# A selective scan on one core: C rows spread by DMA instead of TensorE, one scan over both halves, skip term and residual summed in PSUM

## The reference, cut to what matters

```python
xc, z = split(x @ in_w.T)                       # 256 inner channels each
xc = silu(causal_conv(xc, conv_w) + conv_b)     # 4 taps
dt, Bm, Cm = split(xc @ xp_w.T)                 # 8, 16 and 16 columns
delta = softplus(dt @ dtp_w.T + dtp_b)
def step(h, (u_t, d_t, B_t, C_t)):
    h = exp(d_t[..., None] * A) * h + (d_t * u_t)[..., None] * B_t[:, None, :]
    y = sum(h * C_t[:, None, :], axis=-1)       # over 16 states
y = (scan(step) + xc * Dskip) * silu(z)
out = y @ out_w.T
```

## Time and profile before

| | before |
|---|---|
| median of three runs | 6968.48 us (6958.11 to 6979.99) |
| profiled execution | 6968.54 us, span 6966.8 us, mean PE clock 0.856 |
| busy over the span | PE 5471.0, DVE 4363.1, POOL 3229.9, ACT 2835.7 us |
| scan stage | from 141.65 us (first scan) to 2045.6 us (last skip term), of it DVE busy 93% |

### The profile page before, as it was taken

How to read it: one execution, slowest core, us unless ns; L and a number is a source line. 1 busy time by engine, 2 the same in 40 slices (tenths; PEclk the granted TensorE clock), 3 DMA queues, 4 the chain that set the end, 5 groups by cost and what they waited for, 6 DMA issues and landing times. The chain is left out here.

```text
span 6966.8 us, 82050 instructions
## 1 busy us (share of the span) xinstructions
PE 5471.0 (79%) x22698; PEld 2779.7 (40%) x22762; DVE 4363.1 (63%) x6931; ACT 2835.7 (41%) x4713; POOL 3229.9 (46%) x2381
## 2 busy tenths in 40 slices
PE   4888888888878877798996888853996778784697
PEld 1333333333324344342782444422663333333465
DVE  5999999999985620575224666742675455552575
ACT  4655666666644532354222333421332233341232
POOL 3888888888863400252212333316333344434433
PEclk8999999999999855897557999966997899995898
DMA  1133111111100000000002222212452333211355
GB/s 65 73 134 134 73 73 73 73 73 72 68 36 0 0 0 0 0 0 4 0 0 73 73 69 61 55 74 69 164 190 93 78 72 69 74 27 54 119 188 176
DMA packets 174787, 476.12 MB, mean 68 GB/s; under 512 B 29648, under 2 KB 54992, under 8 KB 146640
## 3 DMA queue, kind: packets, MB, share of 16 engines
q1 hardware_dynamic: 156272, 434.28, 19.5%
q0 software_dynamic: 18176, 37.79, 1.6%
HBM read 364.87 MB, written 107.07 MB: 68 GB/s over the span
## 5 line engine op out<-in xcount | busy, mean ns | idle before, releaser
L337 POOL TENSOR_TENSOR mamba_bu<-mamba_du,mamba_b_all 128x1024 f32<-128x1024 f32 x512 | 1200.5, 2356 | 280.5 <-DVE mamba_hc L599 268.9
L592 DVE TENSOR_TENSOR_SCAN mamba_bu<-psum,mamba_bu 128x512 f32<-128x512 f32 x1024 | 1193.2, 1206 | 157.3 <-ACT psum L529 124.7
L428 PE MATMUL psum<-mamba_hc,consts 128*128 128x512 f32 x2048 | 1017.8, 621 | 31.7 <-DVE mamba_du L604 28.6
L529 ACT ACTIVATE psum<-mamba_delta,A 128x510 f32<-128x510 f32 x1024 | 684.6, 685 | 570.2 <-DVE mamba_bu L592 556.2
L599 DVE TENSOR_TENSOR mamba_hc<-mamba_bu,psum 128x1024 f32<-128x1024 f32 x512 | 611.7, 1195 | 6.1 <-PE psum L419 3.9
L428 PEld LDWEIGHTS psum<-mamba_hc,consts 128*128 128x128 f32 x2048 | 403.6, 198 | 370.3 <-issue 350.9
L1598 POOL DMA_INDIRECT results<-ffn_moe_y_rows,ffn_moe_row_of x312 | 302.1, 968 | 506.4 <-DVE ffn_moe_y_rows L1788 430.8
L2355 POOL TENSOR_TENSOR loc_q_bd<-loc_q_max,weights_l1a 128x512 fp32r<-128x512 f32 x256 | 260.6, 1049 | 585.2 <-DVE loc_q_max L2587 565.5
L1713 ACT ACTIVATE ffn_moe_act<-ffn_moe_act 128x512 f32<-128x512 f32 x344 | 216.9, 630 | 683.4 <-DVE ffn_moe_act L1757 435.6
L2355 POOL TENSOR_TENSOR cau_q_bd<-cau_q_max,weights_l1b 128x512 fp32r<-128x512 f32 x256 | 258.1, 1040 | 448.9 <-DVE cau_q_max L2587 434.1
L2578 DVE TENSOR_REDUCE cau_top<-psum 128x2 f32<-128x512 f32 (+1 forms) x384 | 264.1, 692 | 291.5 <-PE psum L2422 278.6
(11 more groups left out here) (395 smaller groups left out, 11786.3 us busy)
## 6 DMA issues: line engine op xcount, KB each, us to landing
mamba_b_all<-b_rows SPq DMA_DIRECT2D x128, 1024.0 KB
ffn_moe_w_gu<-gate_up_parts SPq DMA_DIRECT2D x78, 1024.0 KB
pairs<-empty_rows SPq DMA_DIRECT2D x6, 3432.0 KB, 15.3
ffn_moe_got<-pairs SPq DMA_DIRECT2D x78, 264.0 KB, 3.3
ffn_moe_w_down<-in_l_moe SPq DMA_DIRECT2D x78, 256.0 KB
qk_rows<-loc_qk SPq DMA_DIRECT2D x16, 1024.0 KB, 10.7
ffn_moe_back<-results SPq DMA_DIRECT2D x32, 512.0 KB, 4.6
qk_rows<-cau_qk SPq DMA_DIRECT2D x16, 1024.0 KB, 4.3
```

Source lines behind the costliest of these rows:

```text
L337: nc.gpsimd.tensor_tensor(bu[:, J % BU, :, :], du[:, q % 2, :, :], b, ALU.mult).then_inc(bu_ready, 1)
L428: nc.tensor.matmul(ysum[h], mem.ident, hc[:, J % HC, h, :], start=(n == 0), stop=(n == NST - 1), skip_group_check=True).then_inc(summed, 1)
L529: nc.scalar.activation(by_seq(dA[i % DECAYS])[:, :, 1:S], by_seq(delta[:, q % 2, h, :])[:, :, 1:S], ACT.Exp, scale=mem.A[:, q % 2, h * NST ...
L592: nc.vector.tensor_tensor_scan(bu[:, J % BU, h, :], dA[i % DECAYS], bu[:, J % BU, h, :], 0.0, ALU.mult, ALU.add).then_inc(scanned, 1)
```

## The change

- B and C rows are both stored to DRAM and both spread by DMA, in chunks of two steps (B and C, 1 MB) into four slots `bc_all`; eight such DMAs per unit instead of four. A slot is refilled when both its steps have been weighed. The bf16 parts, their four instructions per unit and the 16 `spread_c` matmuls per unit go.
- `scan` is one instruction over 1024 elements; both decays of a step lie in neighbouring banks, four banks hold two steps, and a decay waits for the scan two steps back.
- `weigh` multiplies in place in `bu` with C from SBUF; `bu` has eight tiles; `drive` waits for `summed`, the reduce eight steps back.
- The skip term is a matmul with a diagonal matrix `skip` (two per unit, built once) that opens `ysum`; `gated` is one DVE instruction `ysum * z`; POOL's gate goes.
- The residual `X` is added by a matmul with the identity in the bank of the output projection, and ACT evicts straight to `X`; `outp` and POOL's add go. `out` moves from n = 5 to n = 4 on PE.

```diff
             for d, c in enumerate(DIRS):
+                for h in range(HALVES):
+                    nc.vector.tensor_scalar(mem.skip[:, d, h, :], mem.ident, w["D_" + c][:, h:h + 1], None, ALU.mult)
...
-    CHUNK = 4
-    BU, HC, DECAYS = 4, 3, 3
+    CHUNK, SLOTS = 2, 4
+    CHUNKS = NST // CHUNK
+    BU = 8
...
-        b_all = sb("b_all", [NST // CHUNK, CHUNK, T])
+        bc_all = sb("bc_all", [SLOTS, 2, CHUNK, T])
         bu = sb("bu", [BU, 2, T])
-        hc = sb("hc", [HC, 2, T])
-        dA = [mem.bank[i] for i in range(DECAYS)]
-        c_bc = mem.bank[3]
+        dA = mem.psum[:, 0:4, :].rearrange("p (a h) t -> p a h t", a=2)
         work = [mem.bank[4], mem.bank[5]]
-        ysum = [mem.bank[6], mem.bank[7]]
+        ysum = mem.psum[:, 6:8, :]
...
+        def place(J):
+            chunk = J // CHUNK
+            return chunk % SLOTS, J % CHUNK
...
-                sp.dma_start(b_rows[q % 2], xdbl[32:32 + NST, :]).then_inc(b_stored, 16)
-                sp.wait_ge(b_stored, 16 * (q + 1) + LEAD)
-                for c in range(NST // CHUNK):
-                    if q >= 1:
-                        sp.wait_ge(bu_ready, NST * (q - 1) + CHUNK * (c + 1) + LEAD)
-                    rows = b_rows[q % 2, c * CHUNK:(c + 1) * CHUNK, :].rearrange("n t -> (n t)")
-                    sp.dma_start(b_all[:, c, :, :].rearrange("p n t -> p (n t)"),
-                                 rows.unsqueeze(0).to_broadcast([D, CHUNK * T])).then_inc(b_landed[c], 16)
+                sp.dma_start(b_rows[q % 2], xdbl[32:32 + 2 * NST, :]).then_inc(bc_stored, 16)
+                sp.wait_ge(bc_stored, 16 * (q + 1) + LEAD)
+                for c in range(CHUNKS):
+                    chunk = q * CHUNKS + c
+                    if chunk >= SLOTS:
+                        sp.wait_ge(weighed, CHUNK * (chunk - SLOTS + 1) + LEAD)
+                    rows = b_rows[q % 2].rearrange("(a n) t -> a (n t)", a=2)[:, c * CHUNK * T:(c + 1) * CHUNK * T]
+                    sp.dma_start(bc_all[:, chunk % SLOTS, :, :, :].rearrange("p a n t -> p a (n t)"),
+                                 rows.unsqueeze(0).to_broadcast([D, 2, CHUNK * T])).then_inc(bc_landed[chunk % SLOTS], 16)
...
-                    pool.wait_ge(b_landed[n // CHUNK], 16 * (q + 1) + LEAD)
+                    chunk = J // CHUNK
+                    pool.wait_ge(bc_landed[chunk % SLOTS], 16 * (chunk // SLOTS + 1) + LEAD)
                     pool.sem_inc(PASSED[0], 1)
-                pool.wait_ge(hc_ready, J - BU + 1 + LEAD)
+                pool.wait_ge(summed, J - BU + 1 + LEAD)
                 pool.sem_inc(PASSED[0], 1)
-                b = b_all[:, n // CHUNK, n % CHUNK, :].unsqueeze(1).to_broadcast([D, 2, T])
+                slot, row = place(J)
+                b = bc_all[:, slot, 0, row, :].unsqueeze(1).to_broadcast([D, 2, T])
                 nc.gpsimd.tensor_tensor(bu[:, J % BU, :, :], du[:, q % 2, :, :], b, ALU.mult).then_inc(bu_ready, 1)
...
-            def gate(q):
-                d = q % 2
-                pool.wait_ge(z_ready, q + 1 + LEAD)
-                pool.sem_inc(PASSED[0], 1)
-                for h in range(HALVES):
-                    pool.wait_ge(y_step, 2 * q + h + 1 + LEAD)
-                    pool.sem_inc(PASSED[0], 1)
-                    nc.gpsimd.tensor_tensor(du[:, d, h, :], du[:, d, h, :], z[:, d, h, :], ALU.mult).then_inc(y_ready, 1)
-
-            def out(q):
-                pool.wait_ge(work_read, position["out", q, 0] + 1 + LEAD)
-                pool.sem_inc(PASSED[0], 1)
-                nc.gpsimd.tensor_tensor(X[:, tokens(q)], X[:, tokens(q)], outp[:, :], ALU.add).then_inc(added, 1)
-
-            split_rest(0)
-            split_last(0)
             step_size(0)
...
-                    if n == 5 and q >= 1:
-                        gate(q - 1)
-                    if n == 10 and q >= 1:
-                        out(q - 1)
-                    if n == 11 and more:
-                        split_rest(q + 1)
-                    if n == 13 and more:
-                        split_last(q + 1)
                     if n == 15 and more:
                         step_size(q + 1)
-            gate(UNITS - 1)
-            out(UNITS - 1)
...
-            def spread_c(q, n):
-                J = NST * q + n
-                if n == 0:
-                    pe.wait_ge(parts_ready, q + 1 + LEAD)
-                pe.wait_ge(hc_ready, J + LEAD)
-                nc.tensor.matmul(c_bc, mem.sel[:, NST + n:NST + n + 1].to_broadcast([D, D]), parts[:, q % 2, :],
-                                 start=True, stop=True).then_inc(c_ready, 1)
-
             def reduce(J):
                 q, n = J // NST, J % NST
-                pe.wait_ge(hc_ready, J + 1 + LEAD)
+                d = q % 2
                 if n == 0:
-                    pe.wait_ge(y_step, 2 * q + LEAD)
+                    pe.wait_ge(y_ready, q + LEAD)
+                    for h in range(HALVES):
+                        nc.tensor.matmul(ysum[:, h, :], mem.skip[:, d, h, :], u[:, d, h, :], start=True, stop=False, skip_group_check=True)
+                pe.wait_ge(weighed, J + 1 + LEAD)
                 for h in range(HALVES):
-                    nc.tensor.matmul(ysum[h], mem.ident, hc[:, J % HC, h, :], start=(n == 0), stop=(n == NST - 1),
-                                     skip_group_check=True).then_inc(summed, 1)
+                    last = nc.tensor.matmul(ysum[:, h, :], mem.ident, bu[:, J % BU, h, :], start=False, stop=(n == NST - 1),
+                                            skip_group_check=True)
+                last.then_inc(summed, 1)
 
             def out(q):
                 to = claim(("out", q, 0))
+                pe.wait_ge(y_ready, q + 1 + LEAD)
                 for h in range(HALVES):
-                    pe.wait_ge(y_ready, 2 * q + h + 1 + LEAD)
-                    last = nc.tensor.matmul(to, mem.out_proj[:, q % 2, h, :], du[:, q % 2, h, :], start=(h == 0), stop=(h == 1))
-                last.then_inc(work_ready, 1)
+                    nc.tensor.matmul(to, mem.out_proj[:, q % 2, h, :], du[:, q % 2, h, :], start=(h == 0), stop=False, skip_group_check=True)
+                nc.tensor.matmul(by_seq(to), mem.ident, in_time(by_seq(X[:, tokens(q)]), q), start=False, stop=True, skip_group_check=True).then_inc(work_ready, 1)
...
-                    spread_c(q, n)
                     if NST * q + n >= 1:
                         reduce(NST * q + n - 1)
                     if n < 4 and more:
                         convolve(q + 1, n // 2, n % 2)
-                    if n == 5 and q >= 1:
+                    if n == 4 and q >= 1:
                         out(q - 1)
...
-                act.wait_ge(y_step, 2 * (q - 1) + LEAD)
+                if q >= 2:
+                    act.wait_ge(summed, NST * (q - 2) + 1 + LEAD)
...
-                act.wait_ge(parts_ready, q + LEAD)
-                act.wait_ge(b_stored, 16 * q + LEAD)
-                nc.scalar.activation(first[:, :], src, ACT.Identity, scale=w["from_64"]).then_inc(first_ready, 1)
-                nc.scalar.activation(xdbl[:, :], src, ACT.Identity).then_inc(work_read, 1)
-
-            def round_rest(q):
-                act.wait_ge(rest_ready, q + 1 + LEAD)
-                nc.scalar.activation(second[:, :], rest[:, :], ACT.Identity, scale=w["from_96"]).then_inc(second_ready, 1)
...
-                    i = 2 * (NST * q + n) + h
-                    act.wait_ge(scanned, i - DECAYS + 1 + LEAD)
-                    nc.scalar.activation(by_seq(dA[i % DECAYS])[:, :, 1:S], by_seq(delta[:, q % 2, h, :])[:, :, 1:S], ACT.Exp,
+                    J = NST * q + n
+                    act.wait_ge(scanned, J - 1 + LEAD)
+                    nc.scalar.activation(by_seq(dA[:, J % 2, h, :])[:, :, 1:S], by_seq(delta[:, q % 2, h, :])[:, :, 1:S], ACT.Exp,
                                          scale=mem.A[:, q % 2, h * NST + n:h * NST + n + 1]).then_inc(dA_ready, 1)
...
-                act.wait_ge(added, q + LEAD)
-                act.wait_ge(parts_ready, min(q + 2, UNITS) + LEAD)
-                nc.scalar.activation(in_time(by_seq(outp[:, :]), q), by_seq(src), ACT.Identity,
+                nc.scalar.activation(in_time(by_seq(X[:, tokens(q)]), q), by_seq(src), ACT.Identity,
                                      bias=w["proj_b"] if q % 2 == 0 else mem.zero).then_inc(work_read, 1)
...
             def scan(J):
                 dve.wait_ge(bu_ready, J + 1 + LEAD)
-                for h in range(HALVES):
-                    i = 2 * J + h
-                    dve.wait_ge(dA_ready, i + 1 + LEAD)
-                    nc.vector.tensor_tensor_scan(bu[:, J % BU, h, :], dA[i % DECAYS], bu[:, J % BU, h, :], 0.0,
-                                                 ALU.mult, ALU.add).then_inc(scanned, 1)
+                dve.wait_ge(dA_ready, 2 * J + 2 + LEAD)
+                in_row = bu[:, J % BU, :, :].rearrange("p h t -> p (h t)")
```

(21 more changed lines are left out.)

52 lines of the change are left out of this document (14 added, 38 removed).

## The result

The changed kernel takes 7231.45 us (median of 4 runs, 7180.47 to 7251.17) against 6963.86 us beside it: ratio 1.0368 [1.0336, 1.0399]. It is slower, as forecast, but by 268 us where 110 were forecast, and outside the range (6950 to 7200).

A forecast was written before the change was run, and what follows sets the result against it. DVE was taken to bound the scan stage, 59.2 us per unit. The forecast added 3.3 us per unit over 31 units (+102), +10 for fills and -3 once to 6968.5: 7078 us, range 6950 to 7200.

The forecast's parts named there:

- The hold: weigh on DVE and POOL's work, both reading SBUF: one waits for the other in full, except POOL's first 0.15 us.
- term 1: POOL's delta and du run until 3.55 us after the scan of n = 13 starts, delaying weigh: +1.4 us per unit.
- term 2: Behind the skip term POOL goes on out of phase: +1.1 us per unit, absorbed by the wait at n = 7.
- term 3: In the wait at n = 7 POOL starts a further drive: +0.85 us per unit.
- term 4: After a slot's refill the last chunk's drive starts some 1.7 us into a scan: +1.75 us per unit.
- rival A: POOL wins the 0.1 us race against weigh and runs at the landed chunks' edge: +10 us per unit, 7290 us; 12%.
- The sum without a conflict: A unit of the scan stage on DVE without SBUF conflicts: 59.4 us, against 59.2 before.
- The sum with the hold: A unit with DVE and POOL waiting for each other at SBUF: 59.4 + 1.4 + 1.7 = 62.5 us.
- The fills: In six units SP's 3.4 MB fill, 15.3 us, delays the next unit's first drive: +10 us, bounds 0 and 60.
- the case at 3788.54: In a later stage POOL had four queued instructions and DVE got in between two: a waiting DVE goes at POOL's next boundary.
- B: No hold between weigh and POOL, or conflicts fall into DVE's waits: unit 59.4 us, some 6972 us, no change; 13%.
- C: Deeper decay and bu buffers dissolve DVE's waits for ACT: 4.7 us less per unit, 6818 us, faster; 9%.

The follow-up runs named there:

- PE awake: The changed kernel with 50 bf16 matmuls per unit, results unread, added on PE ahead of the waits at n = 0, 7 and 13: 7068.72 us, 1.0149.
- The run without the hold: the control with weigh's second operand from the decays' PSUM banks instead of C in SBUF, product with C left out: 7026.06 us, 1.0071.
- no hold, PE awake: The changed kernel with weigh's second operand from PSUM (product with C left out) and added matmuls filling PE's pauses: 7006.54 us, 1.0028.
- the control: The changed kernel with one added wait on ACT: a decay also waits for the weigh three steps back: 7236.64 us, 1.0377.
- the last run: Kernel before with convolutions ahead of reduce, projections earlier, softplus spread over n = 10 to 12, round_rest at n = 11, split_last at n = 12: 6858.86 us, 0.9854.

## Why the prediction was right in sign and short in size

- **The hold: right as a mechanism, its places only in part.** By the groups `weigh` grew by 1520 - 1196 = 324 ns, 16 times: 5.2 us per unit; terms 1 to 4 together were 1.4 + 1.1 + 0.85 + 1.75 = 5.1. That the two agree is luck. Mean stretches over units 2 to 30: W(12) 1.6 (term 1: 1.4), W(1) 0.9 (term 2: 1.1), W(6) 0.5 (term 3: 0.85), W(9) 1.0 (term 4: up to 1.75), and 1.0 at W(15), which no term has. With PE awake W(9) and W(15) take 1.19, and the waits at S(10) and S(0) are gone with them: nothing is left of term 4, of which the sum had two thirds. The run without the hold confirms the cause.
- **W(15)** is rival A's thin margin, once per unit. In 30 of 31 units the wait of S(0) and the duration of W(15) add up to 3.38 to 3.40 us; in one of them S(0) waited only 0.01 and W(15) took 3.38. In the unit shown POOL's `drive` ran from 1158.01 to 1160.35, begun before `weigh` asked at 1159.00, and `weigh` ended 1.08 behind it; however long S(0) was late, the end is the same. The unit left over, with no wait, has 1.19.
- **The sum without a conflict: right.** 59.4 us was forecast; 60.6 is measured with neither hold nor half clock, 59.7 without the wait that the fillers make. The chain from W(9) to S(13) is 9.4, not 9.1; by the forecast's own terms (9.4 - 0.2 - 0.6 + 0.7) it should have been 9.3.
- **The sum with the hold: right at full clock.** 62.5 us was forecast; 62.4 is measured with the hold and PE awake. The hit within 0.1 us has luck in it: the hold costs some 2.7 there, where 3.1 was forecast, with term 4 at nothing and W(12) larger.

Mean pieces of the unit, worked out from DVE's rows (this table belongs to the points above and below):

| piece | forecast | no hold, PE awake | PE awake | after |
|---|---|---|---|---|
| S(2) to S(7) | 19.1 | 19.2 | 19.3 | 19.8 |
| S(7) to the end of W(9) | 13.3 | 13.3 | 13.9 | 15.9 |
| W(9) to S(13) | 9.1 | 9.4 | 9.4 | 10.6 |
| S(13) to S(2) | 17.9 + 1.4 | 18.6 | 19.7 | 22.1 |
| wait at S(0), S(7), S(10), S(13) | 0, 2.4, 0, not given | 0.84, 2.53, 0, 2.78 | 0, 1.76, 0, 2.66 | 1.12, 2.01, 0.92, 3.89 |

- **The step that failed** is the silent one under all of these: every duration of PE (1.72 us for `reduce`, seven blocks in 12.5 us, the projections) was taken from rows at full clock. The prediction named a half clock only in its last paragraph, as a sign to look for, with no price and no chance. After the change a unit is 68.3 us, 5.8 more than forecast; over 31 units that is 180, the difference between the stage after (2172) and with PE awake (1993). What the runs showed in its place: stretched `weigh`s and late scans lengthen PE's pauses (3.15 us in the kernel before, 6.62 after), PE then runs at half clock for 594 us where before had 167, the convolutions and projections come late to ACT, the next decay is late, DVE waits, and PE's pause grows again. The last two columns of the table differ by some 6 us per unit, in the waits at S(10), S(0) and S(13) and in the stretches of W(9) and W(15). The sign was there to be read in the kernel before: 3.01 us for `reduce` behind a pause of 3.15.
- **The ledger of the stage**, with PE awake: 1888 before, 1932 with the new structure (+44, of which some 26 are the fillers' wait at S(0); the rest is by the units the wait at n = 7, 1.17 to 2.53 us, less 0.8 for sixteen shorter steps), 1993 with the hold (+60, or some 86 against a stage without the fillers' wait), and 2172 at the clock that was granted (+179); less the 12 that the clock costs before: +271. The two causes overlap. Without the hold the change is 211 us faster, with PE awake 168 (against the control), with both 230. So of the hold's 211 us some 60 to 86 are its own (7069 against 7007, and the fillers' 26), and the other 125 to 150 come through PE's pauses.
- **Term 4's lesson was half right**: chunk landings do set the phase in which POOL starts, but finer slots only shift it. A chunk of 1 MB landed in 5.3 us in the median, forecast 4.9. The fills (10 us) were not seen.
- **The rivals.** A did not come as a rule: W(2), W(8) and W(11) are at 1.19 us on average, DVE was served first, as in the case at 3788.54; only at W(15) did POOL get in. B fell with the 1.08 us of the first unit shown. C fell: waits for ACT doubled. The deeper buffers could bring nothing, as the prediction argued, while a decay may not start before the scan two steps back has ended; no run gave the decays more room, so that is not shown. To move ACT's blocks apart does bring something, as the last run shows.

Left open: the fillers were not tried in other numbers, the decays not with more banks, and the spread blocks not in the changed kernel.

## What to carry to other kernels

Before a DVE operand moves from PSUM to SBUF beside a busy POOL, count every overlap of the two as one waiting for the other, and lay POOL's starts out by phase; idle time of POOL does not protect from it. When a sum contains a pause of PE, make it twice, with the durations of rows behind short and behind long pauses, since the stretch that looks like its own price may be the smaller part. Where matmuls fill a pause, fit their number to it: 26 of them outlasted a shorter pause and held `reduce` back by 2.16 us. Where DVE waits for blocks of ACT, cut the blocks and put one piece behind each decay, and move what other engines' queues wait for along with them.

## What was not expected of the hardware

- Fifty matmuls without use per unit made the kernel 163 us faster, with half-clock time going from 594 to 24 us.
- `reduce` takes 1.88 us at full clock, 3.01 behind a pause of 3.15 us that ended in one spread, 3.78 behind pauses of 3.61 and of 6.62.
- POOL is slowed by the hold more than DVE in total: `drive` 3004 ns for 2356, +332 us over 512 instructions, against +167 us on `weigh`. The scan still waited for POOL only 35.6 us, against 32.6.
